# A transformer block on one core: stored rows and staged weights issued in other slots, the feed-forward's row split on GpSimd

## What is computed

```python
h = layernorm(x, ln1_g, ln1_b)
x = attention(h, h, sa_wq, sa_wk, sa_wv, sa_wo, sa_bo) + x
h = layernorm(x, ln2_g, ln2_b)
x = attention(h, cond_emb, ca_wq, ca_wk, ca_wv, ca_wo, ca_bo) + x
h = layernorm(x, ln3_g, ln3_b)
p = h @ ff_w1 + ff_b1
a, gate = p[..., :1024], p[..., 1024:]
return a * gelu(gate) @ ff_w2 + ff_b2 + x
```

## Time and profile before

| | before |
|---|---|
| median of 3 runs | 1755.3 us (1753.64 to 1759.18) |
| the profiled execution | 1751.78 us, its span 1750.0 us |
| granted TensorE clock, mean of the span | 0.998 |
| TensorE, matmuls | 1707.8 us busy, 98% |
| VectorE | 1488.8 us, 85% |
| ScalarE | 1168.9 us, 67% |
| GpSimd | 1050.7 us, 60% |
| DMA | mean 152 GB/s |

### The profile page before, as it was taken

The page is one execution under the profiler, slowest core; times in us unless marked ns, Lnnn a source line. Parts: engine busy times, 40 slices in busy tenths (PEclk is TensorE's granted clock), DMA queues, the critical chain, the costliest instruction groups (busy, mean ns, idle before and its releaser), DMA issues.

```text
span 1750.0 us, 42771 instructions
## 1 busy us (share of the span) xinstructions
PE 1707.8 (98%) x13572; PEld 1663.4 (95%) x13572; DVE 1488.8 (85%) x3216; ACT 1168.9 (67%) x3230; POOL 1050.7 (60%) x1791
## 2 busy tenths in 40 slices
PE   6999999999999999999999999999999998999998
PEld 5999999999999999999999999999999997888887
DVE  6888888888888888889998999999999987676664
ACT  4767777777777777777777777777787775221221
POOL 3778677766666666687777777666666654100100
PEclk9999999999999999999999999999999999999999
DMA  7876677776666666667777777776666662211210
GB/s 199 211 166 167 172 179 173 176 183 167 161 152 156 159 153 159 166 164 183 188 187 186 188 186 174 178 180 168 166 171 166 164 160 54 73 49 61 68 42 24
DMA packets 286447, 265.94 MB, mean 152 GB/s; under 512 B 102416, under 2 KB 244624, under 8 KB 286224
## 3 DMA queue, kind: packets, MB, share of 16 engines
q1 hardware_dynamic: 233552, 250.87, 56.7%
q10 hardware_dynamic: 52672, 12.34, 3.4%
HBM read 70.40 MB, written 24.90 MB: 54 GB/s over the span
## 4 chain that ended last, share of the span: by engine, by line
PE 72%; SPq 7%; POOL 5%; DVE 4%; ACT 4%; issue 4%; DMA 4%; ACTq 1%; POOLq 0%; DVEq 0%
PE QKB L279 15%; PE PVB L335 10%; PE PTB L321 9%; PE WOP L308 8%; PE VB L294 7%; PE S L258 5%; PE S L259 5%; PE S L766 4%; PE PTB L766 4%; ACT PT L414 2%; PE VB L779 2%; PE QKB L779 2%; SPq L1003 2%; SPq L1001 2%; SPq L1020 1%
## 5 line engine op out<-in xcount | busy, mean ns | idle before, releaser
L414 ACT ACTIVATE PT<-S,NM 128x256 f32<-128x256 f32 x1024 | 471.1, 472 | 259.3 <-DVE NM L501 204.0
L489 DVE TENSOR_TENSOR PL<-PTB,PH 128x512 fp32r<-128x512 f32 x512 | 348.9, 682 | 68.2 <-ACT PH L433 63.6
L685 POOL TENSOR_TENSOR ON<-ON,RB 128x256 f32<-128x256 f32 x256 | 188.6, 737 | 275.9 <-DVE ON L512 262.5
L501 DVE TENSOR_REDUCE NM<-S 128x2 f32<-128x512 f32 x512 | 325.9, 677 | 0.1
L433 ACT ACTIVATE PH<-PTB 128x1024 fp32r<-128x1024 f32 x256 | 264.4, 1033 | 70.4 <-PE PTB L321 67.1
L321 PE MATMUL PTB<-IDN,PT 128*128 128x128 f32 x2048 | 266.5, 273 | 5.6 <-DVE PL L489 5.6
L258 PE MATMUL S<-RX 128*128 128x256 f32 x1024 | 258.4, 284 | 12.1 <-ACT PT L414 11.9
L259 PE MATMUL S<-RX 128*128 128x256 f32 x1024 | 257.4, 283 | 0.0
L321 PEld LDWEIGHTS PTB<-IDN,PT 128*128 128x128 f32 x2048 | 229.4, 140 | 7.1 <-DVE PL L489 6.8
L308 PE MATMUL WOP<-WO,OT 128*128 128x256 f32 x1536 | 226.8, 284 | 2.7 <-POOL OT L690 2.7
L279 PE MATMUL QKB<-HT,WA 128*128 128x256 f32 x1536 | 209.9, 287 | 6.6 <-POOL HT L588 3.6
(11 more groups left out here) (107 smaller groups left out, 3090.4 us busy)
## 6 DMA issues: line engine op xcount, KB each, us to landing
RX<-QKS SPq DMA_DIRECT2D x512, 192.0 KB, 2.9
RX<-QKS SPq DMA_DIRECT2D x512, 128.0 KB, 2.8
RB<-denominators SPq DMA_DIRECT2D x512, 64.0 KB, 2.6
out_dram<-XR SPq DMA_DIRECT2D x32, 256.0 KB, 3.0
rows<-XN SPq DMA_DIRECT2D x24, 256.0 KB, 3.0
rows<-HF SPq DMA_DIRECT2D x23, 256.0 KB, 3.0
XR<-in_x_dram SPq DMA_DIRECT2D x16, 256.0 KB, 3.3
denominators<-RDT SPq DMA_DIRECT2D x256, 16.0 KB
```

Source lines behind the costliest of these rows:

```text
L414: last = e.activation(PT[:, c % 2, j * S:(j + 1) * S], S1[:, i, qt * S:(qt + 1) * S], ACT.Exp, bias=NM[:, j:j + 1], accum_out=DEN[:, c % 2 ...
L489: e.tensor_tensor(PL[:, cols], PTB[:, i, :], PH[:, s % 2, cols].bitcast(F32), ALU.subtract).then_inc(a.dve_pl, 1)
L501: e.tensor_reduce(NM[:, i * TT:(i + 1) * TT], S1[:, i, :].rearrange("p (t s) -> p t s", t=TT), AX.X, ALU.max, negate=True).then_inc(a.dve_ ...
```

## The change

Five things are moved.

1. `store_rows` is issued in the same slot as before (pair 0), but behind `spread_den` and ahead of `save_den` and `copy_ring`.
2. The staging of weights (`stage_cross`, `stage_ffn`) is issued where pair is 0, not 1.
3. Of the context's pieces, ScalarE issues piece 0, piece 3 and pieces 6 and 7 ahead of the exponentials of the slots with pair 3, 4 and 5, and pieces 1, 2 and 4, 5 at the end of the first two.
4. The first feed-forward rows: statistics in ATT-16 to ATT-14, normalizing in ATT-11 and ATT-10, one store each in ATT-10 and ATT-9, two loads a slot in ATT-8 to ATT-5 (one on SyncE, one on ScalarE), turns in ATT-4 and ATT-3, both `act_ffn_h` in ATT-2. Each half has semaphores of its own.
5. The rows of chunks 1 to 7 are split by GpSimd (`pool_ffn_split`), and `act_ffn_h` runs in slot 6, not 5. The first chunk's are still split by VectorE.

```diff
-                act_load_ctx(e, seq + 2, *range(3 * (pair - 3), min(3 * (pair - 2), 8)))
+                act_load_ctx(e, seq + 2, *((0,), (3,), (6, 7))[pair - 3])
...
-            if ATT - 3 <= c < ATT - 1:
-                act_ffn_h(e, 0, c - ATT + 3)
+            if ATT - 8 <= c < ATT - 4:
+                load_ffn_rows(e, 0, 2 * (c - ATT + 8) + 1)
+            if c == ATT - 2:
+                act_ffn_h(e, 0, 0)
+                act_ffn_h(e, 0, 1)
...
+            if pair in (3, 4) and sl.has(PAIRS * (seq + 2)) and seq + 2 >= B:
+                act_load_ctx(e, seq + 2, *((1, 2), (4, 5))[pair - 3])
...
+        def load_ffn_rows(e, chunk, *parts):
+
+            for part in parts:
+                h, q = divmod(part, 4)
+                e.wait_ge(d_fs[h], 16 * (chunk + 1))
...
+                load_turned(e, TURNED[h], HS[1 + h, :, :], d_fl[h], q)
...
-            if c >= 0 and c % PAIRS == 5 and sl.has(c + PAIRS):
+            if c >= 0 and c % PAIRS == 6 and sl.has(c + PAIRS):
                 for k in range(KD):
                     act_ffn_h(e, c // PAIRS + 1, k)
...
+        def pool_ffn_split(e, chunk):
+            for k in range(KD):
+                e.wait_ge(fs.act_hf, KD * chunk + k + 1)
+                if k == 0 and chunk > 1:
+                    e.wait_ge(fs.pe_f1, PAIRS * (chunk - 1))
+                e.tensor_copy(rounded(chunk, 0, k), ROWS[k]).then_inc(fs.s_hh, 1)
+                e.wait_ge(fs.s_hh, KD * chunk + k + 1)
+                e.tensor_tensor(rounded(chunk, 1, k), ROWS[k], rounded(chunk, 0, k).bitcast(F32),
+                                ALU.subtract).then_inc(fs.s_ht, 1)
...
                 if f == 2:
+                    sl.wait(e, fs.s_ht, KD * (chunk + 1))
                     dve_normalize(e, sl, fs, chunk + 1, ROWS)
...
-                if f == 6:
-                    dve_ffn_split(e, sl, chunk + 1)
-
...
-            if c == ATT - 11:
+            if c == ATT - 16:
...
-            if ATT - 5 <= c < ATT - 3:
-                dve_ffn_turn(e, 0, c - ATT + 5)
+            if ATT - 4 <= c < ATT - 2:
+                dve_ffn_turn(e, 0, c - ATT + 4)
...
-                if pair == 1 and 1 <= seq <= NCH:
+                if pair == 0 and 1 <= seq <= NCH:
...
-                if pair == 1 and B + 1 <= seq <= B + NCH:
+                if pair == 0 and B + 1 <= seq <= B + NCH:
...
-                if pair == 0 and 0 <= seq < 2 * B - 1:
-                    store_rows(seq + 1)
-                if c == ATT - 6:
-                    store_ffn_rows(0)
-                if c == ATT - 5:
-                    load_ffn_rows(0)
...
             for c in range(-AHEAD, ATT + 2):
                 if c >= 2:
                     spread_den(c - 2)
+                if c % PAIRS == 0 and 0 <= c < ATT - PAIRS:
+                    store_rows(c // PAIRS + 1)
+                if c in (ATT - 10, ATT - 9):
+                    store_ffn_rows(0, c - ATT + 10)
+                if ATT - 8 <= c < ATT - 4:
+                    load_ffn_rows(e, 0, 2 * (c - ATT + 8))
                 if 1 <= c <= ATT:
                     save_den(c - 1)
...
             for chunk in range(1, NCK):
                 pool_rstd(e, zero_ffn, fs, chunk)
+                pool_ffn_split(e, chunk)
                 pool_add_bias(e, zero_ffn, fs, chunk)
```

More of the change, by code:

```diff
@@ L155, in block_kernel @@
         d_hl = sem("d_hl")
-        d_fs = sem("d_fs")
-        d_fl = sem("d_fl")
+        d_fs = [sem(f"d_fs{n}") for n in range(2)]
+        d_fl = [sem(f"d_fl{n}") for n in range(2)]
         d_dup = [sem(f"d_dup{n}") for n in range(2)]
@@ L461, in dve_normalize @@
                 last = e.tensor_scalar(to, rows, MV[:, t, 0:1], RSTD[:, t:t + 1], ALU.subtract, ALU.mult)
-                if t == TT * sl.per - 1:
+                if sl.per == 2 and t % TT == TT - 1 or t == TT * sl.per - 1:
                     last.then_inc(a.dve_xn, 1)
@@ L570, in pool_add_bias @@
         def pool_add_bias(e, sl, a, n, *tiles):
-            sl.wait(e, a.dve_xn, n + 1)
+            sl.wait(e, a.dve_xn, (n + 1) * sl.per)
             for t in tiles or range(TT * sl.per):
@@ L715, in __init__ @@
                 self.dve_th = sem("dve_th_f")
-                self.dve_ch = sem("dve_ch_f")
-                self.dve_ht = sem("dve_ht_f")
+                self.s_hh = sem("s_hh_f")
+                self.s_ht = sem("s_ht_f")
                 self.dve_xo = sem("dve_xo_f")
@@ L754, in pe_ffn @@
                 if f == 0:
-                    sl.wait(e, fs.dve_ht, KD * (chunk + 1))
+                    sl.wait(e, fs.s_ht, KD * (chunk + 1))
                 sl.wait(e, fs.dve_hf, c - 1)
@@ L783, in pe_ffn @@
                 last.then_inc(fs.pe_f2, 1)
+        def load_ffn_rows(e, chunk, *parts):
+            for part in parts:
+                h, q = divmod(part, 4)
+                e.wait_ge(d_fs[h], 16 * (chunk + 1))
+                if chunk:
+                    e.wait_ge(fs.dve_th, 2 * chunk)
+                else:
+                    e.wait_ge(s_pw, 2 * QTR * NCH)
+                load_turned(e, TURNED[h], HS[1 + h, :, :], d_fl[h], q)
         def act_ffn_h(e, chunk, k):
@@ L804, in dve_ffn_turn @@
         def dve_ffn_turn(e, chunk, h):
-            e.wait_ge(d_fl, 128 * (chunk + 1))
+            e.wait_ge(d_fl[h], 64 * (chunk + 1))
             for k in range(KD):
@@ L816, in dve_ffn_split @@
                     sl.wait(e, fs.pe_f1, PAIRS * (chunk - 1))
-                e.tensor_copy(rounded(chunk, 0, k), ROWS[k]).then_inc(fs.dve_ch, 1)
-                sl.wait(e, fs.dve_ch, KD * chunk + k + 1)
+                e.tensor_copy(rounded(chunk, 0, k), ROWS[k]).then_inc(fs.s_hh, 1)
+                sl.wait(e, fs.s_hh, KD * chunk + k + 1)
                 e.tensor_tensor(rounded(chunk, 1, k), ROWS[k], rounded(chunk, 0, k).bitcast(F32),
-                                ALU.subtract).then_inc(fs.dve_ht, 1)
+                                ALU.subtract).then_inc(fs.s_ht, 1)
[4 more added lines that the diff above has]
+                    e.wait_ge(fs.pe_f1, PAIRS * (chunk - 1))
+                e.tensor_copy(rounded(chunk, 0, k), ROWS[k]).then_inc(fs.s_hh, 1)
+                e.wait_ge(fs.s_hh, KD * chunk + k + 1)
+                e.tensor_tensor(rounded(chunk, 1, k), ROWS[k], rounded(chunk, 0, k).bitcast(F32),
+                                ALU.subtract).then_inc(fs.s_ht, 1)
         def dve_ffn(e, sl):
@@ L896, in dve_attention_slot @@
                 dve_weights(e, 2 * c + 5, 1)
-            if c == ATT - 11:
+            if c == ATT - 16:
                 e.wait_ge(a.dve_xo, B + HOLD + 2)
                 dve_stats(e, zero_ffn, fs, 0, 0, 1)
-            if c == ATT - 10:
+            if c == ATT - 15:
                 dve_stats(e, zero_ffn, fs, 0, 2, 3)
-            if c == ATT - 9:
+            if c == ATT - 14:
                 dve_aggregate(e, zero_ffn, fs, 0)
-            if c == ATT - 8:
+            if c == ATT - 11:
                 e.wait_ge(a.pl_ht, 4 * B)
@@ L907, in dve_attention_slot @@
                 dve_normalize(e, zero_ffn, fs, 0, ROWS, (0, 1))
-            if c == ATT - 7:
+            if c == ATT - 10:
                 dve_normalize(e, zero_ffn, fs, 0, ROWS, (2, 3))
-            if ATT - 5 <= c < ATT - 3:
-                dve_ffn_turn(e, 0, c - ATT + 5)
+            if ATT - 4 <= c < ATT - 2:
+                dve_ffn_turn(e, 0, c - ATT + 4)
             if c == ATT - 1:
@@ L916, in pool_attention_slot @@
             pool_slot(e, sl)
-            if sl.c == ATT - 9:
+            if sl.c == ATT - 13:
                 pool_rstd(e, zero_ffn, fs, 0)
@@ L972, in store_rows, with store_ffn_rows @@
                 e.dma_start(HS[0, :, :], near(n)).then_inc(d_hs, 16)
-            def store_ffn_rows(chunk):
-                e.wait_ge(fs.dve_xn, chunk + 1)
-                if chunk:
-                    e.wait_ge(d_fl, 128 * chunk)
-                for h in range(2):
-                    e.dma_start(HS[1 + h, :, :], ROWS[h]).then_inc(d_fs, 16)
-            def load_ffn_rows(chunk):
-                e.wait_ge(d_fs, 32 * (chunk + 1))
-                if chunk:
-                    e.wait_ge(fs.dve_th, 2 * chunk)
-                else:
-                    e.wait_ge(s_pw, 2 * QTR * NCH)
-                for h in range(2):
-                    load_turned(e, TURNED[h], HS[1 + h, :, :], d_fl, 0, 1, 2, 3)
+            def store_ffn_rows(chunk, *hs):
+                for h in hs:
+                    e.wait_ge(fs.dve_xn, 2 * chunk + h + 1)
+                    if chunk:
+                        e.wait_ge(d_fl[h], 64 * chunk)
+                    e.dma_start(HS[1 + h, :, :], ROWS[h]).then_inc(d_fs[h], 16)
             half = DA // 2
@@ L1122, in _ @@
                 if chunk + 1 < NCK:
-                    store_ffn_rows(chunk + 1)
-                    load_ffn_rows(chunk + 1)
+                    store_ffn_rows(chunk + 1, 0, 1)
+                    load_ffn_rows(e, chunk + 1, *range(8))
                 e.wait_ge(fs.dve_xo, PAIRS * (chunk + 1))
```

## The result

| | before | changed |
|---|---|---|
| median of 4 runs each, same chip | 1755.5 us (1753.6 to 1759.2) | 1735.5 us (1732.1 to 1737.8) |
| the profiled execution | 1751.8 us, its span 1750.0 | 1737.8 us, its span 1736.0 |
| granted TensorE clock, mean of the span | 0.998 | 0.998 |

The ratio is 0.9882, with an interval from 0.9859 to 0.9905: the changed kernel is faster by 20.0 us. I had forecast 1739, in a range of 1731 to 1748.

The account below looks back on a forecast made before the run. TensorE was taken as the bound, busy 1707.8 of 1750.0 us. Terms 5.0+9.2+0.6+1.5+3.0-3.1 = 16.2 us off 1751.78 gave 1735.6, plus 3.5 to the median, 1739; range 1731 to 1748.

Parts of the forecast that it names:

- The mechanism of the store: First slot of a sequence: row store issued 3.4 us sooner, exponentials no longer wait for its landing, TensorE's 1.14 us wait goes.
- The median of the runs is 3.5 above that execution, so 1739.: Last step of the sum: 1735.6 us for the profiled execution, plus 3.5 us, gives the forecast median 1739.
- Ten issues in a slot: SyncE in a sequence's first slot: ten issues, 6.2 us in a slot of 5.42, the backlog gone before the third.
- rival b: Attention: SyncE becomes the bound, scores wait for ring copies; half of 14.8 us stays, 1746 to 1747; 14 in 100.
- I cost it at nothing: Staging moved to the first slot: no cost; bad end 0.5 us in each of 12 sequences, 6 us.
- The split: Feed-forward chunk starts: TensorE waits 0.6 us for GpSimd at seven boundaries, 4.2 us; net +3.1.
- 1.1 goes with the old split: Feed-forward: of 1.7 us lost in six chunks before the change, 1.1 us leaves with VectorE's split.
- Rival (a): Feed-forward: GpSimd's 512-wide operations come near their lower bound, the 4.2 us vanish: 1735; 18 in 100.
- (c): Chunk boundaries: GpSimd and VectorE wait for shared memory access, 2.2 us each (15 us); no visible gain, 1751; 7 in 100.
- (d): Chunk boundaries: the same memory sharing at over 3.5 us each makes the kernel slower, 1762; 4 in 100.
- The transition: First feed-forward rows: the 3.5 us wait and slow restart go, 4.2 us, against +0.7 and +0.5; net gain 3.0.
- the start: Slot from 28.64 to 35.94 us, TensorE waiting 1.49 behind the first store: gain between 0 and 2.3, taken as 1.5.

## Why the prediction was right, and what was off

**The mechanism of the store** held step by step: normalized rows, a store 3.3 us sooner, no exponential behind a landing, GpSimd no longer behind the pieces that are staged sooner. The store alone brings as much as the whole change, 1.19% against 1.18 and 1.38% on two chips: what the first feed-forward rows gain (6.2 us alone) the split on GpSimd mostly takes back (3.9).

**What was off is a size, and the step that carried it over: "The median of the runs is 3.5 above that execution, so 1739."** I took those 3.5 us as an offset that the changed kernel would keep. The terms gave 16.2 us; from profile to profile they came to 14.0, and from median to median to 20.0. The difference is the place of the two profiled executions: that of before is 3.7 us under its median (1755.5), that of the changed kernel 2.2 above its own. No term covers these 5.9 us. That the sum for the profiled execution, 1735.6, meets the measured median, 1735.5, is luck: the execution that it was for took 1737.8.

What the runs show in its place is that the late store costs more in other executions than in the one that I read. Take sequences 17 to 23. With the store late they take 313.7 us before, and 314.4 (context pieces), 318.6 (feed-forward rows), 319.6 (staging behind the store) and 322.5 (split) in one profile each of four kernels whose edits leave the late store in them. In the eight kernels with the store early they take 304.6 to 307.1. The landings differ as well: over sequences 18 to 22 the store lands 3.4 us behind its issue in the mean before, 3.7 to 4.2 in those four, and 2.6 with the store alone moved. Part of it is the clock. In the stretch of 322.5 us the granted clock is 0.98, and TensorE is busy for 311.9 us with the matmuls that took 308.1 before. Over whole executions the clock tells the same: the kernel before has 0.993 to 0.996 in its 20 runs beside the store alone, which has 0.996 to 0.998; the profile that I read has 0.998. So the early store brings 7 to 18 us in this stretch, where I had 9.2 for all three edits that bear on it. That the same kernel varies so much from one execution to the next is inferred, since each of these has one profile and they differ in kernel and chip; there is no profile of before on the chips where its median is 1761. Why landings differ stays open.

**Ten issues in a slot** (rival b: half of 14.8 us stays) came true only in small: ScalarE's copy waits for ring copies 16.8 us in all, and at most 0.3 us of a slot in sequences 17 to 22 reach TensorE by it, 1.1 us in the stretch. The two slots of distance hide the rest.

**"I cost it at nothing"**, of the staging's move, was right for this change and would have been wrong by 31 us without the store's: it depends on what stands behind it in the queue. My bad end for it, 6 us, was reckoned from issue times; it missed that the store behind the stage lands later still (4.8 us in the mean, not 3.4) and that the clock falls behind the gaps.

**The split** was forecast at +3.1 us and is +2.4 from profile to profile and 3.9 against the same kernel without it. The two differ because of the term "1.1 goes with the old split": the kernel with the first rows alone still has the old split, and its chunks have lost those waits. Part 4 took them away, by its semaphores of each half as I read it. So the split costs its full price, 4.2 in my working, and part 4 is worth more than its 3.0. In the chain (T+4.5 to T+8.95, 0.6 us a boundary) start and end stood within 0.12 us: T+4.40, T+8.83, 0.5 a boundary. The rows by shape on GpSimd:

```profile
L845 POOL TENSOR_TENSOR PH<-XN,PH 128x512 fp32r<-128x512 f32 x4 | 5.4, 1349 | 0.3
L845 POOL TENSOR_TENSOR PH<-HF,PH 128x512 fp32r<-128x512 f32 x4 | 5.2, 1292 | 0.3
L843 POOL CAST PH<-HF 128x512 fp32r<-128x512 f32 x4 | 4.3, 1070 | 0.0
```

The subtraction takes 1.29 to 1.35 us where I took 1.37, and the first cast 0.61 where I took 0.70. The second cast takes 1.07 beside VectorE's subtraction; that 0.46 is the sharing for which I had 0.2, and it uses up what the others saved. The estimate from the Trainium skill, GPSIMD Engine Reference, section 3.1 (1.27 us for the subtraction), was as near as mine: the trace agrees with either to within 0.08. The sharing could have been read in the trace of before, where VectorE's subtraction, 0.69 us by itself, took 1.11 beside GpSimd's additions, behind the cast that I did quote:

```profile
1557.78 1.11 DVE L838 TENSOR_TENSOR HT<-PT,HT 128x512 fp32r<-128x512 f32 x1
```

Rival (a), in which the split hides, fell. What I had said for it, that VectorE's casts are far from doubling with width, has no row: all of them in the trace of before are 128x512. Rivals (c) and (d) fell too, with their two microseconds and more a boundary.

**The transition** (-3.0 forecast, -3.1 from profile to profile) and **the start** (-1.5, -1.6) were right. The wait and the slow restart were worth the 4.2 us: the slot of 9.60 us is back at 5.42. The slot with the two activations takes 5.31 us where it took 4.81, and what follows it up to the feed-forward 0.7 us more, near the 0.7 and 0.5 that I had set against the gain; that the activations are the cause no run separates, and in the slots with the statistics nothing is lost. Normalizing moved with its cost, as said: 1.0 us left two slots of sequence 31 and 1.2 came up in two of sequence 30, which spreading it over four slots took away. One reading of the change was wrong: the statistics moved five slots, the stores four and three, the loads three to none, and the turns one slot the other way.

## What to carry to other kernels

Read a stall from the queue of the DMA that ends it: what stands ahead of the issue, and who stands behind the one that waits. Where stalls are landings, the one profiled execution is a sample; see where it lies among the runs before carrying its distance to the median over to the changed kernel. An edit that costs nothing behind one issue may cost 31 us ahead of it. Work given to a less busy engine can slow the one that it was taken from: VectorE gave up 15.6 us here and got 8.0 back in slower operations of its own.

## What the runs showed of the hardware

- The 256 KB row store landed later with more queued ahead. Over sequences 18 to 22 its mean from issue to landing was 2.6 us with the store alone moved up, 3.4 to 4.2 behind four ring copies in five kernels, and 4.8 behind the 512 KB of the stage as well. Single landings overlap (3.2 to 4.9 behind the copies, 4.5 to 5.4 behind the stage too).
- VectorE's cast from memory to memory took 0.84 us beside GpSimd's cast and subtraction, not 0.43, its subtraction with both inputs in memory 1.66, not 0.69; GpSimd's cast went from 0.61 to 1.07. VectorE's operation with one input in PSUM took 0.75 us even where it lay wholly beside GpSimd's subtraction. The Trainium skill, GPSIMD Engine Reference, section 1, says that GpSimd's memory interfaces are shared with VectorE, with contention where VectorE's instruction has two inputs in memory or is in a mode that uses two ports. For the subtraction the trace agrees (0.69 to 1.66 us); in which mode the cast ran no run here shows.
- Behind the gap of 3.05 us that ends at 972.26, TensorE's granted clock was 0.50 from 972.00 to 974.00. Over 335 us of this kernel, the one with the staging alone, with six gaps of 1.5 to 4.2 us, it was 0.96 in the mean, and the same matmuls cost 7.4 us more than where it was 1.00.
